# A Fourier block and a gated convolution block: a pair's inverse moved forward, and four convolution matmuls grouped by type

## The reference

```
block 0:  h  = layernorm(x) @ w_te + b_te                 (16 -> 32)
          fc = gelu([Re, Im] of fft2(h) @ w_fc + b_fc)
          x1 = x + real(ifft2(fc as complex)) @ w_tp + b_tp
          d  = gelu(depthwise3x3(layernorm(x1) @ w_fe + b_fe) + b_dw)
          x2 = x1 + d @ w_fp + b_fp
block 1:  q, k, v = conv3x3(layernorm(x2) @ w_hidden, w_qkv)      (16 -> 192)
          o   = irfft2(rfft2(q) * rfft2(k))  on 8x8 patches, 2 heads
          out = x2 + (v * layernorm(o)) @ w_out
```

## Time and profile before

| | |
|---|---|
| median of 3 runs | 252.25 us (252.25 to 252.96) |
| the profiled execution's own time | 253.98 us |
| its span, first to last instruction | 252.2 us |
| PE busy | 225.5 us, 89% |
| DVE busy | 161.0 us, 64% |
| ACT busy | 137.1 us, 54% |
| POOL busy | 75.7 us, 30% |
| mean granted clock of TensorE | 0.947 |

### The profile page before, as it was taken

One profiled execution on the slowest core, in us unless ns is written; L12 is line 12 of the kernel. 1 busy time (PEld: TensorE's weight loads), 2 busy tenths in 40 slices (PEclk: granted clock), 3 DMA queues, 4 the chain that ended last, 5 costly groups with the idle time before them and its releaser, 6 DMA issues.

```text
span 252.2 us, 4917 instructions
## 1 busy us (share of the span) xinstructions
PE 225.5 (89%) x1902; PEld 142.0 (56%) x1902; DVE 161.0 (64%) x302; ACT 137.1 (54%) x290; POOL 75.7 (30%) x69
## 2 busy tenths in 40 slices
PE   7798899889699999858999999999999999999533
PEld 3268333575545756436666667666666676665211
DVE  2995112428319976932469968678786787866872
ACT  2375075504465855415577766756666567665422
POOL 1715300003003000000023665426664256642540
PEclk9979799979799999999999999999999999999955
DMA  6910000000000005989999389999800000000001
GB/s 253 301 20 8 15 6 0 20 3 3 0 3 1 0 0 155 202 185 197 193 183 247 92 157 200 196 194 200 173 0 0 25 0 21 4 0 21 23 0 42
DMA packets 22407, 21.07 MB, mean 84 GB/s; under 512 B 1786, under 2 KB 21130, under 8 KB 22282
## 3 DMA queue, kind: packets, MB, share of 16 engines
q1 hardware_dynamic: 21968, 20.07, 39.1%
q10 hardware_dynamic: 416, 0.69, 0.8%
HBM read 16.58 MB, written 4.02 MB: 82 GB/s over the span
## 4 chain that ended last, share of the span: by engine, by line
PE 74%; DVE 11%; DMA 5%; ACT 5%; issue 2%; POOL 1%; POOLq 1%; SPq 0%; ACTq 0%; DVEq 0%
PE psum L1109 18%; PE psum L1120 13%; PE psum L1049 6%; PE psum L1130 6%; PE psum L972 5%; PE psum L1110 4%; PE psum L1143 3%; PE psum L1005 2%; DMA parts<-tr 2%; PE psum L1154 2%; PE psum L1032 2%; PE psum L947 2%; PE psum L927 2%; DMA arena<-parts 2%; PE psum L957 2%
## 5 line engine op out<-in xcount | busy, mean ns | idle before, releaser
L1109 PE MATMUL psum<-wc,tile 128*128 128x192 f32 x256 | 59.7, 345 | 4.1 <-ACT tile L365 2.7
L524 POOL TENSOR_TENSOR zp<-zp,ln 128x512 f32<-128x512 f32 x15 | 19.2, 1277 | 102.2 <-DVE zp L842 102.2
L1109 PEld LDWEIGHTS psum<-wc,tile 128*128 128x128 f32 x256 | 38.6, 190 | 18.8 <-issue 9.0
L854 DVE TENSOR_TENSOR arena<-psum,arena 128x512 f32<-128x512 f32 x32 | 22.1, 691 | 32.3 <-ACT arena L681 32.2
L1110 PE MATMUL psum<-wc,tile 128*128 128x192 bf16 x128 | 31.5, 246 | 0.0
L365 DVE COPY tile<-arena 128x256 f32<-128x256 f32 x64 | 25.4, 439 | 3.9 <-DMA arena<-parts 3.5
L681 ACT COPY arena<-psum 128x512 f32<-128x512 f32 x32 | 18.8, 586 | 9.1 <-PE psum L1120 9.1
L1049 PE MATMUL psum<-arena,wdw 102*128 102x512 f32 x48 | 21.6, 593 | 0.0
L1130 PE MATMUL psum<-arena,km 128*64 128x256 f32 x128 | 20.9, 404 | 0.8 <-DVE arena L854 0.8
L674 ACT COPY spec<-psum 128x768 f32<-128x768 f32 x16 | 12.8, 799 | 13.6 <-PE psum L1110 13.6
L365 ACT COPY tile<-arena 128x128 f32<-128x128 f32 x64 | 16.7, 314 | 5.7 <-DMA arena<-parts 5.7
(11 more groups left out here) (120 smaller groups left out, 397.1 us busy)
## 6 DMA issues: line engine op xcount, KB each, us to landing
arena<-padded SPq DMA_DIRECT2D x16, 393.0 KB, 10.5
arena<-parts SPq DMA_DIRECT2D x16, 196.5 KB, 9.0
arena<-padded SPq DMA_DIRECT2D x8, 262.0 KB, 10.3
parts<-tr SPq DMA_DIRECT2D x12, 115.5 KB
wq<-w_qkv SPq DMA_DIRECT2D x1, 1296.0 KB, 12.5
padded<-tr SPq DMA_DIRECT2D x2, 528.0 KB, 6.5
arena<-parts SPq DMA_DIRECT2D x8, 131.0 KB, 10.1
xt<-x SPq DMA_DIRECT2D x2, 512.0 KB, 4.7
```

What stands on the lines that cost most here:

```text
L524: pool_link(pool.tensor_tensor(y, y, along(0), ALU.mult))
L854: dve.tensor_tensor(pr[:, m % 2], psum[:, 1024:2048].rearrange("p (q n) -> p q n", q=2)[:, :, 0:256], kh[:, m % 2], ALU.mult).then_inc(pro ...
L1109: mm(dst, tile[:, n % 2, 2 * h + a, :], wc[:, :], start=True, stop=False)
```

## The change

1. The second pair's `inverse_y(1)` is issued right behind `inverse_x(1)`, into banks 6 and 7; its own wait for the `uw` copies goes. The two `keep_warm` matmuls follow it and write bank 3. The depthwise and project steps wait for `x1_done` one by one.
2. ACT makes the squares and square roots of the second pair's first layer norm between and behind the four window copies, before its first Gelu; the switch to Sqrt and back between the Gelus of j = 1 and 2 goes.
3. `channel_major(0)` is issued between `depthwise(4)` and `depthwise(5)`. On DVE `bordered(0)` goes ahead of the two window copies, which stand between the halves of `split(0)`; on ACT the casts of `part` stand one Gelu earlier.
4. In each convolution step the four fp32 matmuls are issued first, then the four bfloat16 ones. Only the first fp32 matmul of each bank carries the start flag.

```diff
         def x1_bank(j):
-            return bank[(4, 5, 2, 3)[j]]
+            return bank[4 + j]
...
-            for j in range(4):
-                act.wait_ge(w_mm, j + 1)
-                if j == 0:
-                    act.wait_ge(m2_mm, 5)
-                w_evac(act.copy, j).then_inc(w_act, 1)
+            act.wait_ge(m2_mm, 5)
+            for h in range(2):
+                for j in (2 * h, 2 * h + 1):
+                    act.wait_ge(w_mm, j + 1)
+                    w_evac(act.copy, j).then_inc(w_act, 1)
+                square(1, 1, (h,))
+            deviation(1, 1)
             for g in range(G2):
                 load_table(ACT.Gelu)
                 for j in range(4 * g, 4 * g + 4):
-                    if j == 2:
-                        load_table(ACT.Sqrt)
-                        square(1, 1)
-                        deviation(1, 1)
-                        load_table(ACT.Gelu)
-                    if j == 6:
+                    if j == 5:
                         part(0, 0, 0)
                         part(0, 0, 1)
                         part(0, 1, 0)
-                    if j == 7:
+                    if j == 6:
                         part(0, 1, 1)
...
-                    for j in (6, 7):
-                        dve.wait_ge(w_mm, j + 1)
-                        w_evac(dve.tensor_copy, j).then_inc(w_dve, 1)
                     dve.wait_ge(tr_zero, 1)
                     bordered(0)
-                    split(0)
+                    for i in range(2):
+                        dve.wait_ge(w_mm, 7 + i)
+                        w_evac(dve.tensor_copy, 6 + i).then_inc(w_dve, 1)
+                        split(0, i)
...
             inverse_x(1)
             pe.wait_ge(wdw_ready, 1)
-            keep_warm(2, km)
+            inverse_y(1)
+            keep_warm(2, km, 3)
...
             depthwise(1)
-            inverse_y(1)
             depthwise(2)
...
             depthwise(4)
+            channel_major(0)
             depthwise(5)
-            channel_major(0)
             depthwise(6)
...
-                    for a in range(2):
-                        for h in range(2):
-                            dst = bank[a][:, HID * h:HID * h + HID]
-                            mm(dst, tile[:, n % 2, 2 * h + a, :], wc[:, :], start=True, stop=False)
-                            last = mm(dst, tile9_bf[:, n % 2, 2 * h + a, :], wc9[:, :], start=False, stop=True)
+                    for first, stationary, moving in ((True, tile, wc), (False, tile9_bf, wc9)):
+                        for a in range(2):
+                            for h in range(2):
+                                last = mm(bank[a][:, HID * h:HID * h + HID], stationary[:, n % 2, 2 * h + a, :], moving[:, :],
+                                          start=first and h == 0, stop=not first, skip_group_check=True)
```

More of the change, by code:

```diff
@@ L723, in normalise, with split @@
                     dve.tensor_tensor(dst[:, xs(h)], xc[:, g, xs(h)], bc(st[:, g, 3, xs(h)]), ALU.mult).then_inc(z_done, 1)
-            def split(g):
+            def split(g, i):
                 dve.wait_ge(tr_mm, 2 * g + 2)
                 for b2 in range(2):
[L728 to L732, removed]
+                    dve.wait_ge(part_act, 4 * g + 2 * i + b2 + 1)
+                    if i == 0:
+                        dve.tensor_tensor(left_of(g, b2), tr[:, g, b2, 1:9, 1:S + 1], part_of(0, b2), ALU.subtract).then_inc(part_dve, 1)
+                    else:
+                        dve.tensor_tensor(part_of(2, b2), left_of(g, b2), part_of(1, b2), ALU.subtract).then_inc(part_dve, 1)
             def bordered(g):
@@ L831, in _ @@
                 if n == 7:
-                    split(1)
+                    for i in range(2):
+                        split(1, i)
                 if n + 1 < 32:
@@ L1011, in inverse_y @@
                 pe.wait_ge(i1_act, 1 + 2 * g)
-                if g == 1:
-                    pe.wait_ge(w_act, 4)
                 for j in range(2 * g, 2 * g + 2):
@@ L1039, in depthwise @@
                     pe.wait_ge(w_act, t4 + 1)
-                    pe.wait_ge(x1_done, 2)
-                    pe.wait_ge(wdw_ready, 1)
+                    pe.wait_ge(x1_done, t4 + 1)
                 else:
@@ L1055, in project @@
                 pe.wait_ge(gelu2, j + 1)
-                if j in (2, 3):
-                    pe.wait_ge(x1_done, j + 1)
                 for t in range(4):
```

## The result

The median of 12 runs is 249.66 us (246.09 to 251.91), against 252.25 (249.45 to 254.76) for 12 runs of the kernel before; the ratio is 0.986, 95% interval 0.981 to 0.991. The forecast of 245.8 (244.2 to 248.6) had the direction right and two and a half times the size (6.5 us less forecast, 2.6 measured). The profiled execution took 251.5 us with a span of 249.7, against 253.98 and 252.2: 2.5 us less. Runs of one kernel spread over 5 us here, in groups that go with the mean granted clock. At the highest clock (0.967 to 0.969) the kernel before took 249.2 to 250.3 us, median 249.8, in eleven runs over the whole study, the changed one 246.1 and 246.3 (0.967) in two: 3.6 us apart, or 3.4 against the two shortest runs of before in the same measurement (249.5 and 249.6).

What follows compares the result with a forecast made beforehand. The prediction took the chain of waits, three quarters of it PE, as the bound, with DMA waits before the loop. Gains of 4.0 us at the first convolution and 2.5 in the loop took 252.25 to 245.8 us, range 244.2 to 248.6.

Steps and rivals of the forecast that it cites:

- Part 4, 29 x 0.086 = 2.5 us: Convolution loop: three bfloat16-to-fp32 changes a step go, saving 0.086 us in 29 of 32 steps, 2.5 us.
- Steps 7 to 9: Loop stretch where convolutions wait for DVE's gather: the gain of three convolutions was forecast to be absorbed.
- The rule of the Trainium skill: Weight loads overlap running matmuls only across different row groups, making the loop's new order worth nothing; the prediction rejected it.
- Part 1: Moving inverse_y(1) takes 1.72 us off PE's path; filled idle time gives windows(0) the full clock, 1.52 us less.
- Part 2: ACT drops two table loads; PE's 0.41 us Gelu wait goes, so windows(1) starts at 81.2.
- Part 3: Earlier channel_major(0): two PE waits for DVE, some 1.1 us; in return part stores at 91.7, taps' loads at 94.2.
- my 2 to 5.1: Bounds for the landing of ACT's part stores: 2 to 5.1 us after the last issue at 97.2.
- The term: Landing of ACT's stores at 101.4, a gain of 4.0 us, putting the first convolution at 107.4.
- Rival (b): ACT's part stores stand behind all the taps' loads, landing only 1 us earlier: 248.7 us; chance 0.08.
- The sum: Whole kernel: 4.0 us at the first convolution plus 2.5 in the loop, 6.5 us less.

Runs made afterwards that it cites:

- before with keep_warm: The kernel before with three more keep_warm matmuls in PE's wait before the first convolution; median 252.63 us, ratio 0.998.
- the order alone: The kernel before with only the loop's new matmul order, four fp32 then four bfloat16; median 248.89 us, ratio 0.979.
- by bank: The kernel before with each convolution's matmuls ordered fp32, fp32, bfloat16, bfloat16, twice over; median 252.46 us, ratio 0.994.

## Why the prediction was wrong, by its own steps

- **Part 4, 29 x 0.086 = 2.5 us: right.** 0.087 a step, 2.4 us from the third step on; the 0.17 of the first two is in their 5.71 us against 5.89 at full clock. Steps 7 to 9 still wait for DVE, as written. The rule of the Trainium skill weighed there ("TensorE: Matmul & The Clock Gate", "Part 3: Packing small matmuls — row/col tiling") does not hold here: weight loads over the same 128 rows were hidden in all three orders, to 29 ns or fully (a 0.11 us load behind a 0.16 us matmul).
- **Part 1: right in the profiled pair.** windows(0) fell by 1.51 us (1.52 written). But I took a low clock that one profile showed for a property of the kernel. Four traces have PE's old order here, with 2.76 to 2.78 us of idle time ahead of windows(0): two (before, and before with keep_warm) ran it at the low clock, two (the order alone, by bank) in 1.92 us. All ten traces with part 1 ran it at the full clock. Runs of before at 0.967 to 0.969 can't have had much of the fall; in those runs the 1.5 us were never there to be gained.
- **Part 2: right.** windows(1) at 81.06 (81.2 written).
- **Part 3: PE's cost right, the return wrong.** The two waits for DVE came at 85.88 and 86.86 (86.0 and 86.9 written), and SP's stores and loads at 91.7 and 94.2, to 0.1 us. I wrote that the loads' early start gives the stores less to wait for. It did the opposite: with the loads ahead of ACT's stores they landed 6.1 us after their issue, outside my 2 to 5.1, two bounds that no row gave. I had the landing follow the end of the taps' bytes, but put that end at about 101 without a row. In the kernel before, the taps' loads took 8.7 us from the first issue to the last landing (99.50 to 108.2), which from 94.2 gives 102.9; it was 102.6. The term was to bring the landing to 101.4; it came at 103.13, and the first convolution at 108.71, not 107.4: 1.3 us. With part 3 undone the same kernel starts its loop 1.6 us sooner after windows(0). Rival (b) had this mechanism, at 0.08, with a price (3.0 at the landing) that was too high.
- **The first steps: the step that was missing.** The sum takes the first convolution's gain over to the end in full, so it leaves the length of the first steps as it was. The wait before it was as long as before (2.75 against 2.67), but lay elsewhere in time and was followed by the lower clock: 2.6 us for two steps. The traces tie it to that wait (six of seven long waits, none of seven short ones, and gone with the wait filled); which run meets it is not settled by anything here, and one kernel with such a wait escaped it in its profile.

Sum: 6.5 - 1.3 - 2.6 = 2.6, and 2.5 were measured in the profiled pair. That the medians are 2.6 apart as well is in part luck: they belong to other runs than the profiled two. At equal clock the change is worth what its parts give without the clock: 2.5 in the loop and, in the start-up, 0.7 (against the order-only trace) to 1.3 (against the by-bank one), near the 3.4 to 3.6 of the runs at the highest clock. Without any low clock the forecast's 6.5 would still have lost the 1.5 of part 1 and the 1.3 of the landing.

## What to carry to other kernels

A schedule that moves work forward moves PE's waits too, and a wait of the same length can meet another clock behind it: fill the waits ahead of the hot loop before its start is tuned, and count in runs, not in one profile, what a low clock costs. When a large load is moved forward, look which small store, on another engine's queue, now stands behind it, who waits for that store, and how long such loads took in the trace at hand from the first issue to the last landing: that is when the store will be there. Where two types of matmul alternate, look for the one whose stream is shorter than the next weight load, and group by type.

## What the runs showed of the hardware

A fp32 weight load of 128 columns behind a bfloat16 matmul of 192 columns costs 29 ns, one, three or no times a step as the order has it (1.681, 1.739, 1.652 us). Three stores of 16.5 KB on ACT's queue took between 3.7 and 6.9 us to land; issued behind 1.05 MB of loads on SP's queue they landed within 0.6 us of the last of these, in six traces. One run of a kernel whose others take 245.4 to 248.2 us took 533 us at a clock of 1.00; it stays unexplained.
